# Moving half of an attention product ahead of the output projection, and two ScalarE steps ahead of their neighbours

## The chip, the cores and the metric

The kernel runs on one core of one Trainium2 chip. The metric is the device time of one execution in microseconds (us), and the median of the runs is compared. Profiles come from the hardware profiler and show one execution each. The engines are TensorE (PE; PEld are its weight loads), VectorE (DVE), ScalarE (ACT), GpSimd (POOL) and SyncE (SP).

## What is computed

The input is 16 sequences of 512 tokens with 128 features, in float32. Six blocks follow one another; each works on a layer norm of x. All cases below are per sequence.

```python
x = x + 0.5 * L0_ffn(layernorm(x))        # one 128x128 product and a bias
x = x + L0_attn(layernorm(x))             # retention, 8 heads, group norm, gate
x = x + 0.5 * L0_ffn(layernorm(x))
x = x + 0.5 * L1_ffn(layernorm(x))        # top 256 of 512 tokens through 128-512-128, GELU
x = x + L1_attn(layernorm(x))             # chunked retention, 4 heads
x = x + 0.5 * L1_ffn(layernorm(x))
```

The change is in the part that computes `L1_attn`:

```python
attn = einsum('bhid,bhjd->bhij', qb, kb) * mask
o = einsum('bhij,bhjv->bhiv', attn, vb) + einsum('bhid,bhdv->bhiv', qb * cross_dec, S)
o = o * rsqrt(mean(o * o) + EPS) * gnorm_w
o = (o * silu(g)) @ Wo.T
```

## The kernel before

**Two phases of slots.** `run_slots` (line 57) writes out a software pipeline over the 16 sequences (batches). The first phase (`slot_a`) does the first three blocks and the routed FFN of all batches; one slot, `slot_ab`, joins the phases; the second phase (`slot_b`, g=17 to 31, then `slot_end`) does `L1_attn` and the last routed FFN. Each engine runs its own list of instructions in the order written, and the lists meet in semaphores. Nothing reorders them: the order in each `slot_b` is the schedule.

**A slot of the second phase** handles three batches at once. For the batch *now* it computes scores, the attention product y and the norm of y. For the batch *new* it prepares queries, keys, values and gates (`sl.prepare`). For the batch *old* it does the output projection and the routed FFN (`sl.complete`; slot 17 has no output projection, since no attention of the second phase lies behind it). A sequence is four chunks of 128 tokens.

**PE in a slot** (line 567): the scores of all four chunks and heads (`scores_b`, L287, banks 0 to 3); the transposes of the gated y of *old* (`transpose_gated`, L547, banks X1 and X2); the part of y carried over from the states of earlier chunks (`carry_b`, L334, banks YB and CB); the values' products of chunks 0 and 1 added to it (`attend_b`, L341, which waits for the chunk's masked scores `msk0` to `msk3`); the output projection of *old* (`output_b`, L555, waits for ACT's copy `gt`); in some slots something for the ranking; the transposes of the new x (`ln_ret`, L255, bank 0); chunks 2 and 3 of the values' products; queries and keys (L260, banks 2 and 3), values (L260); the transposes of h, the normalised x2 of *old* (`ln_mod`, L255, bank X1, waits for `ln_mod_xn`); the transposes of y (`transpose_y`, L564, waits for ACT's copy `ycopy`); the gates' product g_mm (L260, banks X1 and X2, so it waits for `ln_mod_xt`, the copy out of X1); the four up-projections of the routed FFN (`routed_up`, L347) around the transposes of queries and keys (L271); the down-projections (`routed_down`, L353 and L356, bank 2); the new states (`states_b`, L303).

A float32 matmul shows as two PE instructions in the profile, so one `attend_b` (four heads) is 8 of them; a transpose shows as one.

**ACT in a slot** (line 818): the copy gt of the gated transposes (L824); the copy of the `ln_ret` transposes to xt_p (L684); the copy of y to qm (L830); `normalise` (L698, h from x2, waits for DVE's nmr); the copy of the `ln_mod` transposes to xt_r (L684); the values (L734); the squares of the transposed y (L838, waits for `ytok`); the gates' tanh (L741); two GELUs (`hidden`, L688); the copy of queries and keys (L747); two GELUs; the copy of the routed FFN's result (L693).

**DVE in a slot** (line 1354): the four masks over the scores (`causal_b`, L1063); in some slots rank work; x2 from the output projection (`scaled_sum`, L1033); its variance (L1006 to L1019); rank work; nmr (L1024, waits for POOL's root L892); the rotation of queries and keys (L1042, L1043, L1049); h added to the base (L1076); rank work in some slots; the head sums over the squares (`head_sums`, L1087, waits for `sq`); the gate (L1351, waits for `tanh`); the router's sum (L1081); the next input and its variance; the norm of y (L1098) and its gating (L1402, signals `gy`, for which the next slot's `transpose_gated` waits); the states' mask (L1069).

**Ranking.** Every eight batches the router's scores are ranked to choose the 256 tokens of each sequence. This is spread over the slots: a HEAD (18, 26), three ROUNDs of two trials each (19 to 21, 27 to 29), a SPLIT (22, 30), and a WEIGH (23, 31). Slots 17, 24 and 25 have none. In a ROUND slot PE adds up a trial (L385) right after `output_b`, and a second one after the keys, for which it waits for DVE.

**`slot_end`** has no *new* batch. It already runs all four `attend_b` in one go before `output_b`. The serial rest of the last ranking and the stores follow it.

Of the kernel before, what the change touches and what calls it, by code (L numbers as in the profile page):

```python
# [8 lines left out]
ACT = mybir.ActivationFunctionType  # L9
# [6 lines left out]
NB, NT = 16, 4  # L16
# [10 lines left out]
BANK = 512  # L27
# [3 lines left out]
YB, CB, X1, X2 = 4, 5, 6, 7  # L31
# [44 lines left out]
def program(nc, x, xt_d, wq0, wk0, wv0, wg0, wo0, gnw, gnb, kern, bias, fa, fb,  # L76
            wq1, wk1, wv1, wg1, wo1, gcol, wr, w1, b1, w2, b2,
            ident_d, cen_d, tri_d, bd0_d, bd1_d, hm_d, rot0_d, rot1_d, blk_d, rs_d, out):
    with ExitStack() as ctx:
        def sb(name, shape, dt=F32):  # L80
            return ctx.enter_context(nc.sbuf_tensor(name, shape, dt))

        def sem(name):
            return ctx.enter_context(nc.semaphore(name))
# [51 lines left out]
        xt = {n: sb(f"xt_{n}", [P, NT, P]) for n in ("p", "c", "r")}  # L136
# [12 lines left out]
        sq = sb("sq", [P, NT * VF])  # L149
# [9 lines left out]
        PS = ctx.enter_context(nc.psum_tensor("ps", [P, 8 * BANK], F32))  # L159
# [23 lines left out]
        s = {n: sem(n) for n in names}  # L183

        def wait(eng, name, count):
            if count > 0:
                eng.wait_ge(s[name], count)
# [64 lines left out]
        def _(pe):  # L252
# [11 lines left out]
            def tiles(k, width=P):  # L264
                return lambda j: bank(k, j * width, width)
# [17 lines left out]
            def scores_b():  # L283
                for c in range(NT):
                    for g in range(G):
                        rows = slice(32 * g, 32 * g + 32)
                        mm = nc.tensor.matmul(bank(g, c * P, P), qkt[rows, 1, c * P:(c + 1) * P],  # L287
                                              qkt[rows, 0, c * P:(c + 1) * P], start=(c == 0), stop=True,
                                              skip_group_check=True)
                mm.then_inc(s["sc01"], 1)  # L290
# [34 lines left out]
            def head(hd, c):  # L325
                at = (YB + hd // 2) * BANK + c * P
                return PS[hd % 2 * V1:(hd % 2 + 1) * V1, at:at + P]
# [10 lines left out]
            def attend_b(c, sl):  # L338
                wait(pe, f"msk{c}", sl.count(0))
                for hd in range(H1):  # L340
                    mm = nc.tensor.matmul(head(hd, c), vv[sl.buf(0)][:, c, hd * V1:(hd + 1) * V1],  # L341
                                          sc[:, c, hd * P:(hd + 1) * P], start=False, stop=True,
                                          skip_group_check=True)
                mm.then_inc(s["y"] if c == NT - 1 else s[f"av{c}"], 1)
# [198 lines left out]
            def transpose_gated(count):  # L543
                wait(pe, "gy", count)
                for k in range(2):
                    for j in range(NT):
                        mm = nc.tensor.transpose(bank(X1 + k, j * P, P),  # L547
                                                 t2[:, j * VF + k * P:j * VF + (k + 1) * P], ident[:])
                mm.then_inc(s["tg"], 1)
# [9 lines left out]
            def transpose_y(count):  # L559
                wait(pe, "ycopy", count)  # L560
                for c in range(NT):
                    for k in range(2):
                        at = YB * BANK + c * VF + k * P
                        mm = nc.tensor.transpose(PS[:, at:at + P], qm[:, k, c * P:(c + 1) * P], ident[:])  # L564
                mm.then_inc(s["ytok"], 1)

            def slot_b(sl):
                now, new, old = sl.count(0), sl.count(1), sl.count(-1)
                g = sl.g
                wait(pe, "ystore", sl.count(-2))  # L570
                if sl.score:
                    wait(pe, "qm", now)
                    scores_b()
                if sl.score:
                    wait(pe, "um", now)
                if sl.complete:
                    transpose_gated(old)
                if sl.score:
                    carry_b(sl)
                    attend_b(0, sl)  # L580
                    attend_b(1, sl)
                if sl.complete:
                    output_b(old)
                if g in HEAD:
                    rank_rows(HEAD[g], X2)
                if g in ROUND:
                    rank_sum(*ROUND[g], X2)
                if g in WEIGH:
                    rank_mask(WEIGH[g], X2)
                if sl.prepare:  # L590
                    if sl.score:
                        wait(pe, "msk3", now)
                    wait(pe, "x1", new)
                    transpose4("ln_ret", x1[sl.buf(1, 4)], 0)
                if sl.score:
                    attend_b(2, sl)
                    attend_b(3, sl)
                if sl.prepare:
                    wait(pe, "ln_ret_xt", new)
                    tilewise(tiles(2), xt["p"], w_qkv1[:, 0:P])  # L600
                    tilewise(tiles(3), xt["p"], w_qkv1[:, P:2 * P], "qk")
                if g in ROUND:
                    rank_sum(ROUND[g][0], ROUND[g][1] + 1, X2)
                if sl.prepare:
                    tilewise(tiles(0, VF), xt["p"], w_qkv1[:, 2 * P:], "v_mm")
                wait(pe, "ln_mod_xn", old)
                transpose4("ln_mod", h, X1)
                if sl.score:
                    transpose_y(now)
                if sl.prepare:  # L610
                    wait(pe, "ln_mod_xt", old)
                    rank_bank(g)
                    tilewise(tiles(X1, VF), xt["p"], w_g1[:], "g_mm")
                    wait(pe, "v", new)
                wait(pe, "ln_mod_xt", old)
                routed_up(0, 1)
                routed_up(1, 0)
                if sl.prepare:
                    transpose_qk(2, new)
                wait(pe, "act0", old)  # L620
                routed_up(2, 1)
                wait(pe, "act1", old)
                routed_up(3, 0)
                if sl.prepare:
                    wait(pe, "qm", new)
                for f in range(NF):
                    routed_down(f, 2, old)
                if sl.prepare:
                    wait(pe, "gate", new)
                    states_b(X1, sl)  # L630
# [50 lines left out]
        def _(act):  # L681
            def copy_xt(st, dst, k, count):
                wait(act, f"{st}_t", count)
                nc.scalar.copy(dst[:].rearrange("p j n -> p (j n)"), bank(k)).then_inc(s[f"{st}_xt"], 1)  # L684
# [10 lines left out]
            def normalise(count):  # L695
                wait(act, "nmr", count)
                for j in range(NT):
                    last = nc.scalar.activation(h[:, j, :], x2[:, j, :], ACT.Identity, bias=nmr[:, j:j + 1],  # L698
                                                scale=rstd["ln_mod"][:, j:j + 1])
                last.then_inc(s["ln_mod_xn"], 1)  # L700
# [117 lines left out]
            def slot_b(sl):  # L818
                now, new, old = sl.count(0), sl.count(1), sl.count(-1)
                if sl.g in HEAD:  # L820
                    route_weight(HEAD[sl.g])
                if sl.complete:
                    wait(act, "tg", old)
                    nc.scalar.copy(gt[:].rearrange("p k n -> p (k n)"), PS[:, X1 * BANK:(X2 + 1) * BANK]) \  # L824
                        .then_inc(s["gt"], 1)
                if sl.prepare:
                    copy_xt("ln_ret", xt["p"], 0, new)
                if sl.score:
                    wait(act, "y", now)
                    nc.scalar.copy(qm[:].rearrange("p k n -> p (k n)"), PS[:, YB * BANK:(YB + 2) * BANK]) \  # L830
                        .then_inc(s["ycopy"], 1)
                normalise(old)
                copy_xt("ln_mod", xt["r"], X1, old)
                if sl.prepare:
                    values_b(sl)
                if sl.score:
                    wait(act, "ytok", now)
                    nc.scalar.activation(sq[:], PS[:, YB * BANK:(YB + 2) * BANK], ACT.Square).then_inc(s["sq"], 1)  # L838
                if sl.prepare:
                    gates_b(sl)  # L840
                hidden(0, 1, old)
                hidden(1, 0, old)
                if sl.prepare:
                    queries_b(sl)
                hidden(2, 1, old)
                hidden(3, 0, old)
                store_y(2, sl.batch(-1), old)
# [694 lines left out]
```

## Time and profile before

| | us |
|---|---|
| median of 3 runs | 887.64 |
| lowest and highest | 887.13, 889.59 |
| the profiled execution's own time | 889.85 |
| its span in the profile | 888.0 |
| PE busy | 781.9 (88%) |
| DVE busy | 738.3 (83%) |
| ACT busy | 408.3 (46%) |
| POOL busy | 429.0 (48%) |

The span is the profiled part of one execution, from its first to its last instruction; 1.85 us of that execution lie outside it. An engine's busy time leaves out its waits. Matmuls overlap, so a group's duration reaches a little into the next group, and the starts are the better marks. The granted clock of PE is 0.967 of full speed on average; DMA carries 20 GB/s.

### The profile page before, as it was taken

The numbers are of one execution on the slowest core, as the hardware profiler recorded it, in microseconds if no ns is written. First come the engines' busy times: TensorE is split into PE (matmuls) and PEld (weight loads), VectorE is DVE, ScalarE is ACT, GpSimd is POOL, SyncE is SP. The second block draws the span as 40 slices with busy tenths as digits, with TensorE's granted clock in tenths as the row PEclk, the third lists the DMA queues.
The fourth block names the chain that finished last, engine by engine and source line by source line (L and its number), as shares of the span: only waits on it lengthen the run. The fifth ranks groups of instructions, "written<-read, shape, count | busy, mean of one in ns | idle before, by whom it ended". The sixth has DMA issues, their size and how long they took to land.

```text
span 888.0 us, 19163 instructions
## 1 busy us (share of the span) xinstructions
PE 781.9 (88%) x7811; PEld 626.8 (71%) x7811; DVE 738.3 (83%) x1915; ACT 408.3 (46%) x803; POOL 429.0 (48%) x300
## 2 busy tenths in 40 slices
PE   2577899999999899998889999999999999999760
PEld 1456688887777677776678777777788778778540
DVE  2668999999999999998777888887778888896667
ACT  0133445455555455444545455555544445555421
POOL 1346777888878676766633333323322323332210
PEclk9798999999999999999999999999999999999885
DMA  7000000000000000000000000000000000000123
GB/s 190 24 25 25 25 25 25 25 26 25 25 24 25 1 25 25 2 25 24 1 1 2 1 1 2 1 1 1 1 2 1 2 1 1 2 1 1 29 67 94
DMA packets 27226, 18.03 MB, mean 20 GB/s; under 512 B 5361, under 2 KB 24706, under 8 KB 26882
## 3 DMA queue, kind: packets, MB, share of 16 engines
q1 hardware_dynamic: 25378, 16.08, 6.1%
q8 instruction: 62, 1.02, 0.5%
q10 hardware_dynamic: 1760, 0.72, 0.4%
q14 instruction: 26, 0.21, 0.1%
HBM read 12.61 MB, written 4.19 MB: 19 GB/s over the span
## 4 chain that ended last, share of the span: by engine, by line
DVE 46%; PE 40%; POOL 6%; issue 3%; ACT 3%; SPq 1%; DMA 0%; DVEq 0%; ACTq 0%; POOLq 0%
PE ps L260 7%; DVE x L1033 6%; PE ps L356 6%; DVE sc L1055 6%; PE ps L347 6%; PE ps L555 4%; DVE st_ln_mod L1006 3%; PE ps L255 2%; DVE st_ln_f L1006 2%; DVE ra L1042 2%; POOL rstd_ln_f L892 2%; PE ps L341 2%; DVE rb L1043 2%; PE ps L547 2%; DVE t L1283 2%
## 5 line engine op out<-in xcount | busy, mean ns | idle before, releaser
L901 POOL TENSOR_TENSOR grstd<-gve,mhalf 128x32 f32<-128x32 f32 (+1 forms) x32 | 133.9, 4184 | 70.4 <-DVE gve L1092 68.7
L347 PE MATMUL ps<-xt_r,w_s 128*128 128x512 f32 x256 | 130.7, 618 | 1.4 <-ACT xt_r L684 1.4
L356 PEld LDWEIGHTS ps<-w_s,hid 128*128 128x128 f32 x1024 | 121.9, 193 | 9.8 <-issue 8.9
L356 PE MATMUL ps<-w_s,hid 128*128 128x128 f32 x1024 | 125.0, 278 | 0.0
L698 ACT ACTIVATE h<-x,nmr,rstd_ln_mod 128x128 f32<-128x128 f32 x128 | 52.7, 482 | 103.1 <-DVE nmr L1024 103.1
L688 ACT ACTIVATE hid<-ps,b_s 128x512 f32<-128x512 f32 x128 | 88.4, 723 | 14.3 <-PE ps L347 14.0
L892 POOL TENSOR_TENSOR rstd_ln_f<-ve_ln_f,mhalf 128x4 f32<-128x4 f32 x32 | 47.9, 1496 | 88.9 <-DVE ve_ln_f L1019 80.4
L1055 DVE TENSOR_TENSOR sc<-ps,tri 128x1024 f32<-128x1024 f32 x64 | 75.3, 1218 | 7.4 <-PE ps L279 6.6
L892 POOL TENSOR_TENSOR rstd_ln_mod<-ve_ln_mod,mhalf 128x4 f32<-128x4 f32 x32 | 32.9, 1027 | 99.7 <-DVE ve_ln_mod L1019 99.7
L260 PE MATMUL ps<-w_qkvg,xt_p 128*128 128x128 f32 x512 | 67.9, 283 | 0.8 <-ACT xt_p L684 0.8
L684 ACT COPY xt_p<-ps 128x512 f32<-128x512 f32 x32 | 18.8, 587 | 104.4 <-PE ps L255 104.4
L260 PEld LDWEIGHTS ps<-w_qkvg,xt_p 128*128 128x128 f32 x512 | 62.2, 196 | 4.5 <-ACT xt_p L684 3.5
L897 POOL TENSOR_TENSOR r_ret<-ve_ret,powers 128x8 f32<-128x8 f32 x32 | 57.6, 1802 | 15.9 <-DVE ve_ret L1019 15.9
L1033 DVE SCALAR_TENSOR_TENSOR x<-ps,r_ret,x 128x128 f32<-128x128 f32 x128 | 36.0, 344 | 34.0 <-PE ps L555 28.2
L260 PE MATMUL ps<-w_qkv,xt_p 128*128 128x128 f32 (+1 forms) x384 | 62.1, 315 | 0.8 <-ACT xt_p L684 0.8
L347 PEld LDWEIGHTS ps<-xt_r,w_s 128*128 128x128 f32 x256 | 44.1, 196 | 24.4 <-issue 14.8
L916 POOL TENSOR_TENSOR rp<-h,wr_b 128x512 f32<-128x512 f32 x32 | 41.5, 1296 | 35.5 <-ACT h L698 35.5
L260 PEld LDWEIGHTS ps<-w_qkv,xt_p 128*128 128x128 f32 x384 | 52.2, 191 | 6.0 <-issue 3.5
L906 POOL TENSOR_TENSOR um<-um 128x128 f32<-128x128 f32 x32 | 14.6, 457 | 76.6 <-DVE um L1069 76.6
L279 PE MATMUL ps<-qm,qkt 32*128 32x256 f32 x512 | 38.0, 411 | 14.7 <-DVE sc L1055 9.4
L1042 DVE TENSOR_TENSOR ra<-ps,rot 128x1024 f32<-128x1024 f32 x32 | 39.0, 1219 | 13.1 <-PE ps L260 13.1
L693 ACT COPY yall<-ps 128x512 f32<-128x512 f32 x32 | 18.8, 587 | 60.8 <-PE ps L356 60.6
(196 smaller groups left out, 1795.6 us busy)
## 6 DMA issues: line engine op xcount, KB each, us to landing
xin<-in_x SPq DMA_DIRECT2D x16, 256.0 KB, 3.0
xtin<-in_xt SPq DMA_DIRECT2D x16, 256.0 KB, 3.4
out_x<-base SPq DMA_DIRECT2D x16, 256.0 KB, 2.4
rot<-in_rot SPq DMA_DIRECT2D x2, 1024.0 KB, 4.8
w_s<-in_w ACTq DMA_DIRECT2D x2, 256.0 KB, 5.9
w_o<-in_wo ACTq DMA_DIRECT2D x1, 128.0 KB
w_qkv<-in_wv SPq DMA_DIRECT2D x1, 128.0 KB
w_g<-in_wg SPq DMA_DIRECT2D x1, 128.0 KB
```

Source lines behind the costliest of these rows:

```text
L260: mm = nc.tensor.matmul(out_at(j), src[:, j, :], w, start=True, stop=True, skip_group_check=True)
L347: nc.tensor.matmul(bank(k), w1_s[:, f, :], xt["r"][:].rearrange("p j n -> p (j n)"), start=True, stop=True).then_inc(s[f"h{f}"], 1)
L356: mm = nc.tensor.matmul(bank(k, j * P, P), hid[:, f, j * P:(j + 1) * P], w2_s[:, f, :], start=False, stop=(f == NF - 1 and j == NT - 1), s ...
L688: nc.scalar.activation(hid[:, f, :], bank(k), ACT.Gelu_apprx_tanh, bias=b1_s[:, f:f + 1]).then_inc(s[f"act{f}"], 1)
L698: last = nc.scalar.activation(h[:, j, :], x2[:, j, :], ACT.Identity, bias=nmr[:, j:j + 1], scale=rstd["ln_mod"][:, j:j + 1])
L892: nc.gpsimd.tensor_tensor(rstd[st][:], ve[st][:], mhalf[:, 0:NT], ALU.pow).then_inc(s[f"{st}_rstd"], 1)
L897: nc.gpsimd.tensor_tensor(r_ret[sl.buf(1, 4)][:], v, powers[:], ALU.pow).then_inc(s["ln_ret_rstd"], 1)
L901: nc.gpsimd.tensor_tensor(grstd[:, 0:n], gve[:, 0:n], mhalf[:, 0:n], ALU.pow) \
L1006: last = nc.vector.bn_stats(st6[st][:, j, :], src[:, j, :])
L1033: last = nc.vector.scalar_tensor_tensor(dst[:, j, :], bank(k, j * P, P), r[:, j:j + 1], src[:, j, :], ALU.mult, ALU.add)
L1042: nc.vector.tensor_tensor(ra[:], qk, rot[:, 0], ALU.mult)
L1055: nc.vector.tensor_tensor(sc[:, c].rearrange("p (b e n) -> p b e n", b=G, e=2), src.rearrange("p b (e n) -> p b e n", e=2), tri[:].rearran ...
```

## The change

In the second phase's `slot_b`, PE makes the values' products of all four chunks in one run, right behind the carried part and ahead of `output_b`; the transposes of y move from behind the `ln_mod` transposes to the place where chunks 2 and 3 were, behind the `ln_ret` transposes. The wait for `msk3` ahead of the `ln_ret` transposes goes, since `attend_b(3)` has waited for it already. ACT copies y ahead of the `ln_ret` copy, and squares the transposed y ahead of `normalise` instead of behind the values. DVE and POOL are untouched, and so are all other slots.

```diff
@@ PE, slot_b
                 if sl.score:
                     carry_b(sl)
-                    attend_b(0, sl)
-                    attend_b(1, sl)
+                    for c in range(NT):
+                        attend_b(c, sl)
                 if sl.complete:
                     output_b(old)
...
                 if sl.prepare:
-                    if sl.score:
-                        wait(pe, "msk3", now)
                     wait(pe, "x1", new)
                     transpose4("ln_ret", x1[sl.buf(1, 4)], 0)
                 if sl.score:
-                    attend_b(2, sl)
-                    attend_b(3, sl)
+                    transpose_y(now)
...
                 wait(pe, "ln_mod_xn", old)
                 transpose4("ln_mod", h, X1)
-                if sl.score:
-                    transpose_y(now)
                 if sl.prepare:
                     wait(pe, "ln_mod_xt", old)
@@ ACT, slot_b
-                if sl.prepare:
-                    copy_xt("ln_ret", xt["p"], 0, new)
                 if sl.score:
                     wait(act, "y", now)
                     nc.scalar.copy(qm[:].rearrange("p k n -> p (k n)"), PS[:, YB * BANK:(YB + 2) * BANK]) \
                         .then_inc(s["ycopy"], 1)
+                if sl.prepare:
+                    copy_xt("ln_ret", xt["p"], 0, new)
+                if sl.score:
+                    wait(act, "ytok", now)
+                    nc.scalar.activation(sq[:], PS[:, YB * BANK:(YB + 2) * BANK], ACT.Square).then_inc(s["sq"], 1)
                 normalise(old)
                 copy_xt("ln_mod", xt["r"], X1, old)
                 if sl.prepare:
                     values_b(sl)
-                if sl.score:
-                    wait(act, "ytok", now)
-                    nc.scalar.activation(sq[:], PS[:, YB * BANK:(YB + 2) * BANK], ACT.Square).then_inc(s["sq"], 1)
```

## Rows read from the trace of the kernel before

**Rows 1.** The page's busy line: us, share of the span, instructions

```profile
PE 781.9 (88%) x7811; PEld 626.8 (71%) x7811; DVE 738.3 (83%) x1915; ACT 408.3 (46%) x803; POOL 429.0 (48%) x300
```

**Rows 2.** Stretches from one `output_b` to the next: us, engines' busy us (instructions), clock, DMA

```profile
578.17:603.42 25.25, 23.57 (x235) 19.19 (x234) 22.16 (x48) 12.61 (x23) 7.71 (x6) 1.00 0.01 2
603.42:627.60 24.18, 23.88 (x239) 19.62 (x238) 18.91 (x43) 12.62 (x23) 7.71 (x6) 1.00 0.00 1
627.60:651.70 24.10, 23.44 (x234) 19.18 (x234) 18.60 (x41) 12.62 (x23) 7.70 (x6) 1.00 0.01 1
799.33:824.40 25.07, 24.76 (x255) 20.51 (x254) 16.50 (x31) 12.62 (x23) 6.09 (x5) 1.00 0.01 2
```

**Rows 3.** Timeline of slot g=24: start, us, engine, line, operation, count, idle before

```profile
629.62 1.13 DVE L1033 SCALAR_TENSOR_TENSOR x<-ps,r_ret,x 128x128 f32<-128x128 f32 x4 [2.33 <-PE ps L555]
...
629.95 1.09 PE L341 MATMUL ps<-sc,va 128*64 128x128 f32 x16
630.05 0.59 ACT L684 COPY xt_p<-ps 128x512 f32<-128x512 f32 x1 [3.24 <-PE ps L255]
...
633.71 1.65 ACT L698 ACTIVATE h<-x,nmr,rstd_ln_mod 128x128 f32<-128x128 f32 x4 [1.61 <-DVE nmr L1024]
...
635.41 0.66 PE L255 MATMUL ps<-ident,h 128*128 128x128 f32 x4 [0.66 <-ACT h L698]
...
635.80 0.91 PEld L564 LDWEIGHTS ps<-ident,qm 128*128 128x128 f32 x8
...
636.10 0.59 ACT L684 COPY xt_r<-ps 128x512 f32<-128x512 f32 x1 [0.75 <-PE ps L255]
...
636.74 1.59 PEld L260 LDWEIGHTS ps<-w_g,xt_p 128*128 128x128 f32 x8
...
638.02 1.05 ACT L838 ACTIVATE sq<-ps 128x1024 f32<-128x1024 f32 x1
...
638.93 1.61 ACT L741 ACTIVATE t<-ps,r_ret 128x256 f32<-128x256 f32 x4
...
646.19 1.23 DVE L1402 TENSOR_TENSOR t<-t,gate 128x1024 f32<-128x1024 f32 x1
...
648.77 1.09 PE L547 MATMUL ps<-ident,t 128*128 128x128 f32 x8
...
649.90 1.01 ACT L824 COPY gt<-ps 128x1024 f32<-128x1024 f32 x1 [2.33 <-PE ps L547]
```

**Rows 4.** Waits from 480 to 800 us: us in total, times, longest

```profile
DVE gve L1087 <- ACT sq L838: 5.6, 9, 0.7
...
PE ps L385 <- DVE rankb L1160: 4.6, 6, 1.1
...
PE ps L255 <- ACT h L698: 3.7, 7, 0.7
```

**Rows 5.** Timeline of the last slot, PE only: the run of all four chunks

```profile
822.43 1.97 PE L341 MATMUL ps<-sc,va 128*64 128x128 f32 x32
```

**Rows 6.** Timeline of slot g=17, which has no `output_b`

```profile
457.77 1.09 PE L341 MATMUL ps<-sc,va 128*64 128x128 f32 x16
...
460.41 3.78 PE L260 MATMUL ps<-w_qkv,xt_p 128*128 128x128 f32 x24
460.52 1.01 ACT L830 COPY qm<-ps 128x1024 f32<-128x1024 f32 x1 [0.45 <-PE ps L341]
```

**Rows 7.** The chain that ended last, in slot g=24: start, us, what

```profile
638.74 1.72 PE ps L347 x4
...
641.33 1.82 PE ps L347 x4
```

**Rows 8.** Timeline of slot g=22, where DVE has rank work

```profile
580.27 1.13 DVE L1033 SCALAR_TENSOR_TENSOR x<-ps,r_ret,x 128x128 f32<-128x128 f32 x4 [0.77 <-PE ps L555]
...
600.44 1.09 PE L547 MATMUL ps<-ident,t 128*128 128x128 f32 x8 [0.94 <-DVE um L1069]
```

**Rows 9.** A stretch of the tail, `routed_up` (L347) alone: PE, PEld busy us, clock, DMA

```profile
852.20:856.10 3.90, 3.78 (x4) 1.17 (x4) 0.51 0.17 50
```

## The prediction, made before the changed kernel was run

> **What bounds the kernel now.** I read the busy line first, then the table of stretches cut at each start of `output_b`, then the timeline of one ordinary slot, then the waits and the chain. TensorE (PE) is busy 88% of the span [rows 1]. The edit touches only the 15 slots of the second phase, g=17 to 31. Cut from one `output_b` to the next they take 24.1 to 25.3 us, with PE busy 23.4 to 24.8 of it and its clock granted in full [rows 2]. So in this phase a microsecond of PE is a microsecond of the kernel, unless PE is waiting there anyway. The places where it waits have to be known exactly.
>
> The slot whose `output_b` starts at 627.60 us (g=24, no rank work) shows them [rows 3]. `output_b` ends about 629.59. From there a chain runs off PE: VectorE (DVE) sums x2 at 629.62, takes its variance, GpSimd (POOL) the root, and ScalarE (ACT) normalises from 633.71 to 635.36. PE has run the `ln_ret` transposes, the products of chunks 2 and 3 (629.95), the queries, keys and values, and still stands idle for 0.66 us before it can transpose h at 635.41. This wait occurs in 7 of the 13 slots of 480 to 800 us; in the six with two rank rounds PE waits instead for DVE's second rank trial, 0.8 us each on average, which also hangs on x2 [rows 4]. Whatever PE does between `output_b` and the transposes of h is therefore not what sets the time: **`output_b` is**. Its end starts the chain, and everything ahead of it in the slot pays in full.
>
> One more place matters. `transpose_y`'s weight loads last from 635.80 to 636.71. ACT's copy of the `ln_mod` transposes out of bank X1 ends at 636.69, and g_mm, which overwrites X1 and waits for that copy, loads its first weights at 636.74 [rows 3]. So today `transpose_y` fills the time of the copy almost to the tenth.
>
> **The change, part by part.**
>
> *Chunks 2 and 3 ahead of `output_b`.* The same 16 PE instructions (two passes for each of eight matmuls) go from behind `output_b` to before it. A run of 16 lasts 1.09 us [rows 3]; one unbroken run of 32, which the last slot already makes, lasts 1.97 [rows 5]. The difference, 0.88, is what lands ahead of `output_b`. The table gives the same in another way: slots 23 and 31 do the same kind of rank work, and what follows 31 has all four chunks ahead of `output_b`. They take 24.18 and 25.07, a difference of 0.89 [rows 2]. I take 0.89. No mask wait is added to it: the two masks of chunks 2 and 3 are ready when PE comes to them, as in the last slot, whose run of 32 shows no idle. ACT's copy gt, for which `output_b` waits, ends at 650.91, 0.79 before `output_b` starts at 651.70, so it does not start to bind [rows 2, 3].
>
> The Trainium skill (TensorE: Matmul & The Clock Gate, Step-by-step: what each phase is for) says that weight loads can be pulled ahead of running matmuls; were every change between kinds of matmul free by that, nothing would be saved by joining two runs, the 16 instructions would cost the full 1.09 wherever they stand, and the sum below would come out at 15.8 instead of 13.0. The trace does not agree: its run of 32 is 0.21 shorter than two runs of 16.
>
> *What this saves behind `output_b`:* nothing. DVE, POOL and ACT need the same time up to h (or up to the rank trial), and PE arrives early today. `transpose_y` takes the place of the products as cover for the `ln_ret` copy: that copy ends 0.69 us after its cover starts (629.95 to 630.64), and `transpose_y` offers 0.94 (635.80 to 636.74) [rows 3]. PE reaches the wait for h about 0.1 sooner and waits 0.1 longer.
>
> *`transpose_y` taken out between the `ln_mod` transposes and g_mm:* also nothing. From 635.41 to 636.74 it is transposes, copy and wake-up, which remain 1.33 us, now with some 0.9 of PE idle. The work has moved to a place that was free, and left a hole where it had been useful.
>
> *y copied first.* In slots 18 to 31 y is complete as `output_b` starts; ACT finished gt before and copies y (1.0 us) while PE spends 2.0 in `output_b`. No wait. What queues behind it on ACT is the `ln_ret` copy, needed only after `output_b`. In slot 17 there is no `output_b`. There PE starts the products at 457.77, so they end 1.97 later, at 459.74, and y's copy runs to about 460.80. `transpose_y`, with 0.95, then holds the queries back from 460.41 to about 461.79: **+1.4** [rows 6]. h isn't late there: squares would end at about 463.0 and the normalising at 464.6, while PE's queries, keys and values, 3.78 us of them, last to 465.6.
>
> *Squares first.* ACT can square about 2.6 us after `output_b` ends and normalises 4.1 after it, so the square of 1.05 fits. It leaves the stretch between values and gates. The gates then wait for g_mm instead, which ends near 638.75 by the pace of its group, against a start at 638.93 now: 0.15 sooner [rows 3]. ACT's first GELUs follow, and the second pair of `routed_up`, which takes 1.82 against 1.72 for the first, should lose that 0.10 of waiting [rows 7]. In the nine slots that are neither paced by DVE nor otherwise late (17, 19, 20, 23 to 25, 27, 28, 31): **-0.9**. DVE starts its head sums up to 0.71 earlier there, but then waits for the gates, so only 0.15 reaches `gy`. `gy` is no limit in an ordinary slot: it ends at 647.42 and PE asks at 648.77 [rows 3].
>
> *The slots where DVE sets the pace* (g=18, 22, 26, 30, those with the longest rank work). In 22 DVE waits 0.77 for `output_b`, then works through to `um`, for which PE idles 0.94 [rows 8]. This chain starts at the end of `output_b`, so the 0.89 counts here as well; the gap before g_mm and the early squares don't.
>
> **Sum.** 14 slots of 0.89 are 12.5; slot 17 adds 1.4; the relief takes 0.9: +13.0. No DMA, POOL or SP instruction is moved. Behind slot 31 comes serial rank work and the stores, which nothing hides, so the sum reaches the end. On the profiled execution (889.85 us outside, span 888.0) this gives 902.9. The median of the three runs is 2.2 below that execution, and I put the forecast on the median: 887.64 + 13.0 = **900.6**.
>
> Bounds: with the moved run at its full 1.09 and no relief it is 14 x 1.09 + 1.4 = 16.7, that is 904.3. If the hole before g_mm turns out 0.1 shorter, as `transpose_y`'s last load may hold g_mm now, 1.5 goes: 899.1.
>
> **Rivals.**
>
> *The DVE-bound slots take the cost in* (897.0). If the four slots with long rank work had slack at `output_b`, 4 x 0.89 = 3.6 would vanish. DVE's 0.77 of idle in front of x2 speaks against it: it waits for PE there, and would wait longer.
>
> *Faster, by the early squares* (about 882). DVE waits 5.6 us for sq in 9 of 13 slots [rows 4]. If head sums, root and `gy` set when the next slot's transposes begin, those 5.6 would come off, and the products moved forward would cost nothing, as PE would be waiting for `gy` anyway. It decides once `gy` comes later than the end of the scores. In ordinary slots it is 1.35 us ahead; where DVE is late, it has no wait for sq to lose.
>
> *The run is hidden anyway* (889.0, no change). Were gt the last thing before `output_b`, 0.79 of each 0.89 would be covered and 0.10 x 14 = 1.4 left. The rows give that 0.79 as slack and not as waiting.
>
> *The clock falls* (927.6). PE gets a hole of 0.9 us in each slot. Four passes of `routed_up`, 1.72 to 1.82 here [rows 7], take 3.78 in the tail where the granted clock is 0.51, that is 1.2 GHz [rows 9]; g_mm at twice its 1.8 in 15 slots would be +27 on top of the 13. But PE had 1.7 us of idle in slot 22's 25.25 and the granted clock stayed 1.00, that is 2.4 GHz [rows 2].
>
> The Trainium skill (TensorE: Matmul & The Clock Gate, What's actually happening) says that the slow clock is the default state and that activity lifts it, so a rule against any order with more idle in it; here the trace shows the idle of slot 22 at full clock.
>
> *Still more is held up* (905 or more): the squares or y's copy hold up `ln_ret`'s copy or h in every slot. The slack of 1.5 us on ACT before h speaks against it.
>
> **How the numbers follow.** The forecast 77%, DVE slots 10%, faster 4%, hidden 3%, clock 3%, more held up 3%. The range takes in the forecast's bounds and the DVE-slot case: 896.5 to 904.3. A change of 0.3%, 2.7 us, is about what a measurement of this kernel can tell from none. Slower by more than that: 77 + 10 + 3 + 3 = 93%; within it 3%; faster 4%.
>
> **What would show it.** In the profile after: one PE run of 32 (L341) of about 1.97 before each `output_b`, a PE idle of 0.8 to 0.9 before g_mm released by ACT's xt_r, the wait for h or for the rank trial a tenth longer, ordinary slots of about 24.9, DVE no longer waiting for sq, the clock still 1.00. The forecast is wrong if h is transposed sooner after `output_b` than 5.8 us, if g_mm starts sooner than 1.3 after these transposes, or if ordinary slots stay at 24.1.

## The result, and the profile after

The changed kernel takes 901.66 us (median of 4 runs, 901.15 to 903.94) against 887.38 beside it: a ratio of 1.0161, 95% interval 1.0137 to 1.0186, or about 14.3 us more. The forecast was 900.6, slower. A second set of runs of both gave 902.49 against 888.03, 1.0156 (1.0132 to 1.0180).

The page of the changed kernel shows nothing of it but the span (the profiled execution took 901.79); the busy line answers to [rows 1]:

```profile
span 900.0 us, 19148 instructions
...
PE 780.8 (87%) x7811; PEld 630.1 (70%) x7811; DVE 736.9 (82%) x1915; ACT 410.8 (46%) x803; POOL 428.4 (48%) x300
```

Every engine does what it did, and 12 us more pass. The stretches from one `output_b` to the next answer to [rows 2] (us, then the busy us of PE, PEld, DVE, ACT and POOL, the granted clock, DMA):

```profile
581.87:607.98 26.11, 23.38 (x235) 19.19 (x234) 21.30 (x46) 12.82 (x23) 7.70 (x6) 1.00 0.01 2
607.98:632.92 24.94, 23.70 (x239) 19.62 (x238) 18.79 (x43) 12.82 (x23) 7.69 (x6) 1.00 0.01 1
632.92:657.79 24.87, 23.26 (x235) 19.18 (x234) 18.50 (x41) 12.83 (x23) 7.69 (x6) 1.00 0.00 1
784.17:810.81 26.64, 24.95 (x234) 20.26 (x234) 21.47 (x46) 12.93 (x23) 7.69 (x6) 0.94 0.01 2
810.81:835.75 24.94, 23.70 (x238) 19.62 (x238) 16.39 (x31) 12.82 (x23) 6.09 (x5) 1.00 0.00 1
```

Slot 24 went from 24.10 to 24.87, slot 23 from 24.18 to 24.94, slot 22 from 25.25 to 26.11. Slot 31, behind which the last slot always had all four chunks ahead of `output_b`, went from 25.07 to 24.94: it alone got shorter. Slot 30 stands out, 26.64 with the clock at 0.94; of that below.

The timeline of slot g=24 (start, duration, engine, line) answers to [rows 3]:

```profile
632.85 2.05 PE L555 MATMUL ps<-w_o,gt 128*128 128x128 f32 x16
632.97 1.01 ACT L823 COPY qm<-ps 128x1024 f32<-128x1024 f32 x1 [1.71 <-PE ps L341]
...
634.94 1.13 DVE L1028 SCALAR_TENSOR_TENSOR x<-ps,r_ret,x 128x128 f32<-128x128 f32 x4 [3.21 <-PE ps L555]
635.07 0.90 PEld L564 LDWEIGHTS ps<-ident,qm 128*128 128x128 f32 x8
...
635.38 0.59 ACT L679 COPY xt_p<-ps 128x512 f32<-128x512 f32 x1 [1.40 <-PE ps L255]
...
636.25 1.02 ACT L829 ACTIVATE sq<-ps 128x1024 f32<-128x1024 f32 x1 [0.29 <-PE ps L564]
...
639.04 1.65 ACT L693 ACTIVATE h<-x,nmr,rstd_ln_mod 128x128 f32<-128x128 f32 x4 [1.76 <-DVE nmr L1019]
...
640.74 0.66 PE L255 MATMUL ps<-ident,h 128*128 128x128 f32 x4 [0.94 <-ACT h L693]
...
641.43 0.58 ACT L679 COPY xt_r<-ps 128x512 f32<-128x512 f32 x1 [0.75 <-PE ps L255]
...
642.07 1.99 PE L260 MATMUL ps<-w_g,xt_p 128*128 128x256 f32 x8 [0.67 <-ACT xt_r L679]
...
644.10 1.57 ACT L736 ACTIVATE t<-ps,r_ret 128x256 f32<-128x256 f32 x4 [0.61 <-PE ps L260]
```

Read it from `output_b`. It starts at 632.92 (the start of its stretch above), and h is transposed at 640.74: 7.82 later. Before, it was 635.41 - 627.60 = 7.81 [rows 2, 3]. (Both marks lie 0.07 behind the first matmul of `output_b`, which starts at 632.85 here and started at 627.53 before.) So nothing that was taken out of this span shortened it; PE's idle ahead of h grew from 0.66 to 0.94. From 640.74 to the first weight load of g_mm, at 642.07 like its first matmul, it is 1.33, as before, now with 0.67 of idle that ACT's xt_r releases. The squares, at 636.25, are long done before normalising. The gates start 3.36 behind the transposes of h, against 3.52 before.

The waits from 480 to 800 us answer to [rows 4] (us in total, times, longest):

```profile
PE ps L260 <- ACT xt_r L679: 7.4, 11, 0.7
...
PE ps L385 <- DVE rankb L1155: 6.3, 6, 1.3
DVE gate L1346 <- ACT t L736: 5.6, 9, 0.7
PE ps L255 <- ACT h L693: 5.6, 7, 1.0
```

DVE's wait for sq is gone, and one for the gates (5.6) has taken its place. PE's waits for the rank trial and for h grew from 4.6 and 3.7 to 6.3 and 5.6, and the hole before g_mm (7.4) is new.

**Where to measure.** The first phase is the same code in all kernels, yet the scores of slot 17 begin anywhere between 451.9 and 456.6 us in the profiled executions. The stretch from the scores of slot 17 to those of the last slot holds exactly what is edited, and repeats better than the whole. The timeline of PE has its two ends, in the kernel before:

```profile
454.73 1.17 PE L287 MATMUL ps<-qkt 32*128 32x128 f32 x32
...
819.49 1.17 PE L287 MATMUL ps<-qkt 32*128 32x128 f32 x32
```

and in the changed kernel:

```profile
453.17 1.17 PE L287 MATMUL ps<-qkt 32*128 32x128 f32 x32
...
830.84 1.17 PE L287 MATMUL ps<-qkt 32*128 32x128 f32 x32
```

So 364.76 became 377.67: **+12.91**. The second profiled execution of the changed kernel gave 377.66. Below, "the stretch" is this span.

### The profile page after: what moved, and what is told of

Its sections match the earlier page's. It is cut to its first block, busy times and chain, and to the rows that moved or that the text cites. A ratio compares the mean times of both kernels' runs of the same rounds, so it can differ in the third digit from the quotient of the medians.

```text
span 900.0 us, 19148 instructions
## 1 busy us (share of the span) xinstructions
PE 780.8 (87%) x7811; PEld 630.1 (70%) x7811; DVE 736.9 (82%) x1915; ACT 410.8 (46%) x803; POOL 428.4 (48%) x300
## 3 DMA queue, kind: packets, MB, share of 16 engines
q8 instruction: 62, 1.02, 0.5%
## 4 chain that ended last, share of the span: by engine, by line
DVE 44%; PE 41%; POOL 6%; ACT 4%; issue 3%; SPq 1%; DMA 0%; DVEq 0%; ACTq 0%; POOLq 0%
PE ps L260 8%; DVE x L1028 6%; PE ps L356 6%; DVE sc L1050 6%; PE ps L347 6%; PE ps L555 4%; PE ps L341 3%; DVE st_ln_mod L1001 3%; POOL rstd_ln_f L887 2%; DVE ra L1037 2%; DVE rb L1038 2%; DVE st_ln_f L1001 2%; PE ps L255 2%; PE ps L547 2%; DVE t L1278 2%
## 5 line engine op out<-in xcount | busy, mean ns | idle before, releaser
L347 PE MATMUL ps<-xt_r,w_s 128*128 128x512 f32 x256 | 129.5, 612 | 1.3 <-ACT xt_r L679 1.3
L683 ACT ACTIVATE hid<-ps,b_s 128x512 f32<-128x512 f32 x128 | 86.5, 702 | 15.7 <-PE ps L347 14.2
L347 PEld LDWEIGHTS ps<-xt_r,w_s 128*128 128x128 f32 x256 | 44.5, 198 | 23.5 <-issue 15.6
L901 POOL TENSOR_TENSOR um<-um 128x128 f32<-128x128 f32 x32 | 14.5, 454 | 85.7 <-DVE um L1064 85.7
```

Of the source, the lines that this page charges most:

```text
L347: nc.tensor.matmul(bank(k), w1_s[:, f, :], xt["r"][:].rearrange("p j n -> p (j n)"), start=True, stop=True).then_inc(s[f"h{f}"], 1)
L683: nc.scalar.activation(hid[:, f, :], bank(k), ACT.Gelu_apprx_tanh, bias=b1_s[:, f:f + 1]).then_inc(s[f"act{f}"], 1)
```

## The experiments

All ran against the kernel before on the same chip. Its median differed a little from set to set: 889.96 beside e1 to e4, 888.03 beside e5 to e8, 889.14 beside e9 to e11. The expectations reckon from about 887.5, so they are best compared with the results by the ratio or by the stretch. The columns are the median, the ratio with its 95% interval, the stretch in the profiled execution and its difference from 364.76.

| run | us | ratio | stretch | difference |
|---|---|---|---|---|
| changed kernel | 901.66 | 1.0161 (1.0137 to 1.0186) | 377.67 | +12.91 |
| e8 changed kernel again | 902.49 | 1.0156 (1.0132 to 1.0180) | 377.66 | +12.90 |
| e1 four ahead, nothing else | 902.64 | 1.0143 (1.0124 to 1.0163) | 377.57 | +12.81 |
| e2 three ahead | 895.09 | 1.0063 (1.0046 to 1.0080) | 371.01 | +6.25 |
| e3 one ahead | 882.94 | 0.9932 (0.9906 to 0.9957) | 358.82 | -5.94 |
| e4 none ahead | 883.67 | 0.9924 (0.9900 to 0.9947) | 356.75 | -8.01 |
| e11 none ahead, again | 882.60 | 0.9930 (0.9911 to 0.9950) | 356.67 | -8.09 |
| e5 transposes and squares early only | 902.53 | 1.0160 (1.0130 to 1.0190) | 378.49 | +13.73 |
| e9 transposes early, squares late | 890.09 | 1.0008 (0.9995 to 1.0021) | 366.21 | +1.45 |
| e6 changed kernel, hole filled | 903.97 | 1.0173 (1.0156 to 1.0190) | 380.25 | +15.49 |
| e7 changed kernel, squares late | 902.38 | 1.0163 (1.0139 to 1.0187) | 378.55 | +13.79 |
| e10 none ahead, gt in halves | 875.80 | 0.9854 (0.9836 to 0.9872) | 352.45 | -12.31 |

Two theories were tested. A, that of the prediction: the end of `output_b` starts the chain that sets the slot, so what stands ahead of it is paid. B: the cost is the hole that `transpose_y` left before g_mm.

**e1, e2, e3, e4: how many chunks stand ahead of `output_b`.** The edit of e1, in PE's `slot_b` alone:

```diff
                     carry_b(sl)
                     attend_b(0, sl)
                     attend_b(1, sl)
+                    attend_b(2, sl)
+                    attend_b(3, sl)
...
                     transpose4("ln_ret", x1[sl.buf(1, 4)], 0)
                 if sl.score:
-                    attend_b(2, sl)
-                    attend_b(3, sl)
+                    pass
```

The wait for `msk3` ahead of the `ln_ret` transposes stays in e1, though the expectation says that it goes; `attend_b(3)` has waited for it already, so it holds nothing up. e2, e3 and e4 keep it too, and put chunks 0 to 2, chunk 0, or none there, and the rest behind the `ln_ret` transposes.

> Only the products of chunks 2 and 3 go ahead of output_b (and the wait for msk3 with them); transposes of y, the y copy and the squares stay where they were before. Theory A (the end of output_b sets the slot; PE idles before h anyway): 14 slots x 0.89 = 12.5, slot 17 +0.5 because the ln_ret copy loses its cover there: 900.4. No idle before g_mm, but the wait for h grows by 0.3 or so. Theory B (the hole before g_mm, left by the transposes of y, is the cost): the transposes of y fill it here, so at most the uncovered ln_ret copy is paid, and the time stays within 887 to 890.

> Chunks 0, 1 and 2 ahead of output_b, chunk 3 behind, everything else as before. Theory A: half of the step, 0.45 in each of 14 slots, 6.2 in all: 893.7. Theory B (hole before g_mm): no hole opens, 887.4.

> The step in the other direction: only chunk 0 ahead of output_b, 1 to 3 behind. Theory A: 0.45 less in each of 14 slots, out of the 0.66 that PE idles before h: 881.2. A rival, that PE's own work bounds the slot and not the chain from output_b: no gain, 887.4.

> All four chunks behind output_b. Theory A: output_b now waits for ACT's copy gt, so it starts 0.67 earlier and not 0.88; in ordinary slots PE reaches h late and only the idle of 0.66 less the new wait of 0.2 is gained, 0.45 a slot; in the four slots paced by DVE 0.67: 10 x 0.45 + 4 x 0.67 = 7.2, 880.2. If the gain went on in a straight line it would be 12.5, 874.9; if PE's work bounds, 887.4 or above.

Measured, by the stretch: +12.81, +6.25, 0 (two ahead, the kernel before), -5.94, -8.01. One chunk is worth 6 us in either direction until none is left. In e3, PE's idle ahead of h in slot 24 has shrunk from 0.66 to 0.22. e1 has no hole before g_mm, and costs the same as the whole change. This settles it against B. The waits of e1 from 480 to 800 us show where the time stands:

```profile
PE ps L260 <- ACT xt_p L685: 8.8, 13, 0.7
PE ps L385 <- DVE rankb L1161: 6.3, 6, 1.3
PE ps L255 <- ACT h L699: 5.7, 7, 1.0
```

PE waits 0.7 in each slot for the `ln_ret` copy, which has lost its cover, and still waits for h and for the rank trial behind that. PE is idle at another place than in the changed kernel, for as long. The new hole is not what e1 pays for: e3 has none, and gains as much for one chunk moved back as one moved forward costs.

e4's last step gives 2.1 instead of 6, as `output_b` now waits for gt. Its timeline:

```profile
624.59 1.01 ACT L824 COPY gt<-ps 128x1024 f32<-128x1024 f32 x1 [2.33 <-PE ps L547]
...
625.66 2.05 PE L555 MATMUL ps<-w_o,gt 128*128 128x128 f32 x16 [0.29 <-ACT gt L824]
...
627.75 1.13 DVE L1033 SCALAR_TENSOR_TENSOR x<-ps,r_ret,x 128x128 f32<-128x128 f32 x4 [1.66 <-PE ps L555]
...
628.08 1.97 PE L341 MATMUL ps<-sc,va 128*64 128x128 f32 x32
```

0.29 us of idle in each slot. I had put this wait at 0.2, and expected -7.2. Slot 24 gains 0.65 (23.45 instead of 24.10 from scores to scores), where I had 0.45: the expectation left out that all four chunks now make one run, which is 0.21 shorter than two. In e4's waits none for h is left, so PE's own work and its wait for gt now bound the ordinary slots.

**e5 and e9: the transposes early.** e5 leaves the products where they were. `transpose_y` goes behind the keys' product (which leaves ACT the time to copy y), and the squares ahead of `normalise`. e9 is the same with the squares back behind the values:

```diff
@@ PE
                     tilewise(tiles(3), xt["p"], w_qkv1[:, P:2 * P], "qk")
+                if sl.score:
+                    transpose_y(now)
...
                 transpose4("ln_mod", h, X1)
-                if sl.score:
-                    transpose_y(now)
@@ ACT, e5 only
+                if sl.score:
+                    wait(act, "ytok", now)
+                    nc.scalar.activation(sq[:], PS[:, YB * BANK:(YB + 2) * BANK], ACT.Square).then_inc(s["sq"], 1)
                 normalise(old)
                 copy_xt("ln_mod", xt["r"], X1, old)
                 if sl.prepare:
                     values_b(sl)
-                if sl.score:
-                    wait(act, "ytok", now)
-                    nc.scalar.activation(sq[:], PS[:, YB * BANK:(YB + 2) * BANK], ACT.Square).then_inc(s["sq"], 1)
```

> The other half of the change alone: chunks 2 and 3 stay behind output_b, the transposes of y move ahead to behind the keys' product, and ACT squares ahead of normalising. Theory A: the transposes take 0.9 out of an idle of 0.66 (before h) or 0.8 (before the second rank trial) and leave a hole before g_mm that the copy needed anyway: about 0.2 in 10 slots, 0.9 in slot 17, less 0.9 of relief by the early squares: 889.4. Theory B (the hole before g_mm is the cost): 15 x 0.9 = 13.5, 901.

That missed by 13 us. Taken alone the number would have spoken for theory B. The chain of slot g=24 in e5 shows what I had overlooked (start, duration, what):

```profile
637.21 0.89 PE ps L564 x8
...
638.12 1.02 ACT sq L834
639.14 1.54 ACT h L698 x4
...
640.73 0.67 PE ps L255 x4
...
641.42 0.59 ACT xt_r L684
```

The squares wait for the transposes, and ACT, which takes its work in order, can't normalise until it has squared. h begins at 639.04 in its timeline, 1.1 later than DVE and POOL allow. Hence e9:

> The run before it (transposes of y and squares early) came out at +14 where 889.4 was expected: in its trace the squares wait for the transposes, which stand behind the keys, and hold normalising up by 1.1 us in a slot. Here the transposes stay early and the squares go back behind the values. If the squares ahead of normalising were the cause, normalising again starts 4.1 after output_b ends, and only the 0.2 in 10 slots and 0.9 in slot 17 remain, with no relief: +3, about 891, and the stretch from the scores of slot 17 to those of the last slot is 368 (before: 364.8; the run before: 378.5). If the hole before g_mm costs its 0.9 after all, it stays at +13, 901.

It came out at +1.45, its ratio no different from 1. Its waits have the hole before g_mm at full size:

```profile
PE ps L260 <- ACT xt_r L684: 7.4, 11, 0.7
...
PE ps L385 <- DVE rankb L1160: 0.2, 1, 0.2
```

7.4 us of idle in 11 slots, the same as in the changed kernel, and it costs almost nothing, because the work that left it filled the idle ahead of h. Of the 1.45, 0.86 is slot 17 (22.35 from scores to scores instead of 21.49), which I had put at 0.9. The ordinary slots 24 and 25 take 24.11 instead of 24.10 and 24.12; the rest is 0.32 to 0.36 more in each of slots 18, 23, 26 and 31, less 0.37 in each of 19 and 27.

**e6: the hole filled.** In the changed kernel, the values of tiles 2 and 3 move behind the transposes of h, where they cover ACT's copy:

```diff
-                    tilewise(tiles(0, VF), xt["p"], w_qkv1[:, 2 * P:], "v_mm")
+                    values_of((0, 1))
                 wait(pe, "ln_mod_xn", old)
                 transpose4("ln_mod", h, X1)
                 if sl.prepare:
+                    values_of((2, 3)).then_inc(s["v_mm"], 1)
                     wait(pe, "ln_mod_xt", old)
```

> The changed kernel, with the second half of the values' product (0.9 us of PE) moved from ahead of the ln_mod transposes to behind them, where it covers ACT's copy. The hole before g_mm closes. Theory A: PE stands idle before h longer instead, by the same amount, and only slot 17 gains: 901.0 (the changed kernel: 901.7). Theory B (the hole is the cost): 14 x 0.8 = 11 less, 890.

No gain, as A has it. The idle moved in front of h (all waits of PE there from 480 to 800 us):

```profile
PE ps L255 <- ACT h L700: 16.0, 13, 1.9
PE ps L385 <- DVE rankb L1162: 6.3, 6, 1.3
```

16.0 us in 13 slots, longest 1.9. Slot 17 gains 0.53 (22.11 against 22.64 in e8), as A has it. But the time is 1.5 higher than that of the changed kernel beside it (e8, below), and the stretch 2.6; slots 28 and 29 are 26.95 and 26.74 from scores to scores, against 25.48 and 25.43 in e8. PE's waits in slot 28, and the stretches of time in which the loss arose, with the granted clock in the third column from the end:

```profile
740.53 0.18 PE L385 MATMUL ps<-rankb,blkb 128*128 128x1 bf16 x1 [1.34 <-DVE rankb L1162]
...
742.41 1.12 PE L255 MATMUL ps<-ident,h 128*128 128x128 f32 x4 [0.73 <-ACT h L700]
```

```profile
741.00:745.00 4.00, 3.27 (x12) 2.51 (x11) 3.96 (x5) 1.94 (x5) 1.27 (x1) 0.65 0.00 0
745.00:750.00 5.00, 5.00 (x22) 3.48 (x21) 2.85 (x5) 4.33 (x11) 2.90 (x1) 0.94 0.01 3
...
770.00:774.00 4.00, 4.00 (x13) 3.21 (x12) 3.61 (x6) 1.92 (x6) 0.51 (x2) 0.64 0.00 0
774.00:777.00 3.00, 3.00 (x14) 1.78 (x13) 1.42 (x2) 3.00 (x7) 2.69 (x1) 1.00 0.00 0
```

The granted clock was 0.65 of full speed over these 4 us, so it stood at 1.2 GHz for part of them and at 2.4 for the rest, and it was back a few us later. It fell behind two waits of PE, for the second rank trial (1.34, in slot 29 0.99) and for h (0.73 in both). It did not fall behind the longest waits: in slot 24 PE waits 1.80 for h in one piece at a clock of 1.00. Slots 28 and 29 together lost 2.8 us. Without that, and without the 0.5 that a fall of the clock cost e8, e6 would be 0.3 above e8: an estimate, and far from the 11 us less that B asks for.

**e7: the squares.** The changed kernel with only the squares put back behind the values.

> The changed kernel with the squares back behind the values. Theory A: the relief of 0.1 in nine slots is lost, 902.6; DVE waits for sq again. A rival, that the early squares bring nothing at all: 901.7. A rival, that they help DVE's chain: above 905.

The median can't tell this apart (902.38 against 902.49 for e8 beside it). The stretch does: 378.55 against 377.66, +0.89. DVE waits for sq again:

```profile
DVE gve L1082 <- ACT sq L833: 5.7, 9, 0.7
```

So the early squares are worth the 0.9 us that the prediction gave them, in one profiled execution of each. Both executions have one fall of the clock, in slot 22, at the same cost (26.64 and 26.63), so it does not enter the difference. The 0.9 lies where the prediction put it: 0.09 to 0.11 in each of slots 17, 19, 20, 23 to 25, 27, 28 and 31, counted from `output_b` to `output_b` (slot 17 from scores to scores), and at most 0.01 elsewhere.

**e8: the changed kernel again.**

> The changed kernel itself, beside the others on the same chip: 901.7, and the interval of slot 30 shows whether its extra 0.5 us and the tail's extra 0.6 us come back: if they do, they belong to the change, if not to the execution.

Slot 30 is ordinary this time: slots 30 and 31 together take 24.94 + 26.10 = 51.04 from scores to scores. But slots 22 and 23 take 26.63 + 24.94 = 51.57, the 0.5 more that slots 30 and 31 had in the first profile. So the extra 0.5 moves from slot to slot and belongs to the execution. Where it sits, the clock had fallen, here as in the first profile. Three stretches of slot 30 there: the one before g_mm, g_mm's and the one behind it:

```profile
790.00:793.30 3.30, 1.70 (x9) 0.99 (x7) 3.10 (x4) 2.19 (x6) 1.35 (x2) 1.00 0.00 0
793.39:796.80 3.41, 3.41 (x9) 2.73 (x10) 3.38 (x4) 1.42 (x4) 0.00 (x0) 0.56 0.00 0
796.80:799.00 2.20, 2.20 (x9) 1.05 (x8) 2.10 (x4) 2.13 (x6) 0.00 (x0) 0.91 0.00 0
```

g_mm takes 3.44 instead of 1.99 there. DVE paces that slot, so all but 0.5 of the loss is hidden: in slot 22 of the same profile PE waits 1.04 for `um` ahead of the transposes of the gated y, in slot 30 not at all. The tail's extra 0.6 came back: behind the scores of the last slot there are 69.2 and 69.1 us in the two executions of the changed kernel, against 68.5 before. But this part, the same code in all kernels, takes anything from 67.7 (e10) to 69.2 (e9, e4) in the profiles, so one or two executions don't show that it belongs to the change.

In steps of 5 us from 460 to 820, the clock stays at 1.00 in the kernel before and in e1, e2, e3, e4, e5, e9 and e11; e10 has one step of 0.95 at its end, in the tail. It falls once in each profile of the changed kernel and in e7, each time behind waits of 1.0 for h and 0.7 for xt_r, and twice in e6, behind the waits shown above. What makes it fall is not shown: slot 22 of the first profile has the same two waits as its slot 30 (1.01 and 0.67) at 1.00, slots 19 to 21 and 27 of e6 have the same 0.99 and 0.73 as its slot 29 at 1.00, and e5 waits for h and then for xt_r in every slot from 18 on (0.4 to 0.9, then 0.7) without a fall.

**e10: better than both.** e4 leaves one wait, for gt. ACT now copies bank X1 and bank X2 one after the other, and `output_b` takes the first half of each token's features for all four tiles, then the second. The start flag stands on the first matmul into the bank alone, instead of once for each tile. All four chunks stand behind `output_b`, as in e4. The edit against e4:

```diff
@@ ACT
-                    nc.scalar.copy(gt[:].rearrange("p k n -> p (k n)"), PS[:, X1 * BANK:(X2 + 1) * BANK]) \
-                        .then_inc(s["gt"], 1)
+                    for k, name in ((0, "gt_half"), (1, "gt")):
+                        nc.scalar.copy(gt[:, k, :], bank(X1 + k)).then_inc(s[name], 1)
@@ PE, in place of output_b
+                wait(pe, "gt_half", sl.k)
+                for k in range(2):
+                    if k == 1:
+                        wait(pe, "gt", sl.count(-1))
+                    for j in range(NT):
+                        mm = nc.tensor.matmul(bank(X1, j * P, P), gt[:, k, j * P:(j + 1) * P], w_o1[:, k, :],
+                                              start=(k == 0 and j == 0), stop=(k == 1), skip_group_check=True)
+                mm.then_inc(s["wo"], 1)
```

> All four chunks behind output_b, where PE waits 0.27 for gt in each slot. ACT copies gt in two halves (bank X1, then X2), and output_b takes all four tiles' first halves, then the second ones, so it can start when the first copy is done. Theory A: the wait goes, 0.27 in 14 slots, 3.8 less than with one copy: the stretch from the scores of slot 17 to those of the last slot 353 instead of 356.8, the time near 879. If ACT's second copy comes late or PE is bound elsewhere: no gain.

> All four chunks behind output_b, once more beside the version with two copies: stretch 356.8 as before, ratio to the kernel before 0.991 to 0.993.

The stretch is 352.45, 4.2 less than e11's 356.67, and the time 875.8: 13 us below the kernel before beside it, whose median was 889.14; by the ratios it is 3% below the changed one. Its timeline in slot 24:

```profile
621.84 0.89 PE L334 MATMUL ps<-qkt,um 64*64 64x128 f32 x24
621.95 1.07 ACT L835 COPY gt<-ps 128x512 f32<-128x512 f32 x2 [2.33 <-PE ps L547]
...
622.66 2.05 PE L565 MATMUL ps<-w_o,gt 128*128 128x128 f32 x16
...
624.75 1.12 DVE L1043 SCALAR_TENSOR_TENSOR x<-ps,r_ret,x 128x128 f32<-128x128 f32 x4 [1.31 <-PE ps L565]
...
625.07 1.97 PE L341 MATMUL ps<-sc,va 128*64 128x128 f32 x32
```

`output_b` starts 0.82 behind the carried part, with no idle of PE. Two copies of 512 columns take 1.07 together, against 1.01 for one of 1024. The median dropped by more (6.8 against e11) than the stretch. The two profiled executions differ by 4.3, like the stretch; the other 2.5 are not explained.

## Why the prediction was right

- **The sum.** It was worked out for the part from slot 17 on as +13.0; the stretch gave +12.91 and +12.90. That the two are so near is in part luck. Both profiles contain about 0.5 us of a fall of the clock, which the sum had put at nothing. Without it 12.4 are left, 0.6 less than the sum: its largest term, 14 slots of 0.89, measured 0.86 each, 12.0 instead of 12.5, and slot 17 a little less than 1.4. The medians moved by 14.3, in an interval of 12.2 to 16.5, which holds both the 13.0 and the 12.9; what they moved beyond the stretch is not explained. The two profiled executions differ by only 11.9, since the first phase was 1.6 us longer in the one before (454.73 against 453.17), though its code is the same.
- **0.89 ahead of `output_b`.** Confirmed in place, and nearly in size: +0.85 to +0.86 from `output_b` to `output_b` in slots 18, 21, 22, 26 and 29, and 0.76 to 0.77 in 19, 20, 23 to 25, 27 and 28, where the relief comes off. That a run of 32 is 0.21 shorter than two of 16 decided between 13.0 and 15.8. The Trainium skill (TensorE: Matmul & The Clock Gate, Step-by-step: what each phase is for) says that weight loads are pulled ahead of running matmuls. That every change between kinds of matmul is free by this was my own extension of it, and the 0.21 speaks against it here.
- **Nothing saved behind `output_b`.** From the start of `output_b` to the transposes of h it is 7.82 against 7.81. This was the step on which the sign depended, and e1 to e4 confirm it by moving the run and nothing else. PE's extra wait for h was mis-sized, 0.28 (0.94 less 0.66) where the prediction has 0.1, but as idle it costs nothing.
- **The hole before g_mm is free.** 1.33 before and after; e9 and e6 show it from both sides.
- **Slot 17.** 22.64 from scores to scores against 21.49: +1.15, where the working gives 1.4 less 0.1.
- **The squares.** e7 against e8 gives 0.10 a slot in the nine slots named, and 0.89 in all for the predicted 0.9. DVE's gain was taken up by a wait for the gates, as predicted.
- **The DVE-paced slots** pay in full: +0.86 in slot 22. That rival falls.
- **The clock.** The rival had 3% and a price of 27 us for a fall in each slot, and the forecast expected a clock of 1.00 throughout. That is wrong in a detail: the clock does fall, but once in 15 slots, at a cost of 0.5 us in a slot that DVE paces (in e6 1.5 and 1.3 in slots 28 and 29). I had taken slot 22's idle at full clock as reason enough. The Trainium skill (TensorE: Matmul & The Clock Gate, What's actually happening) says that activity lifts the slow clock. The direction agrees: each fall in these profiles came behind waits of PE, and the clock rose again with PE busy. Why one slot in 15 falls and the others, with the same waits, do not stays open.

What I got wrong lies behind the prediction: in e5 I moved ACT's squares without asking what they wait for and who is queued behind them. Without e9, e5's number would have spoken for theory B by accident.

## What to carry to other kernels

Find where the chain that sets the period leaves the busiest engine, here at the end of `output_b`, and look at both sides of it. Work ahead of that point costs its full length and work behind it is free until the chain's answer is waited for, however full the engine looks in total; so the same products that cost 12.8 us when moved forward brought 8.0 when moved back, and 12.3 once the next wait, for gt, was gone too. An engine that takes its work in order must not be given an early step whose input comes late, as e5's squares did.

## What the runs showed that I had not expected

- The granted clock fell in the middle of a phase in which PE was 93% busy: 0.56 over 3.4 us in slot 30 of the changed kernel, right after PE had waited 1.02 for h and 0.68 for xt_r (g_mm 3.44 instead of 1.99). It came back within the slot. In e1 PE idles as much, at other places, and in e5 at the same places, and the clock stays at 1.00.
- One unbroken run of 32 small matmuls takes 1.97, against 1.09 for each of two runs of 16 (the weight loads stand idle 0.17 before each of these runs and behind it). Four chunks in one run take 1.97 wherever they stand: ahead of `output_b` in the changed kernel, behind it in e4.
- DVE and POOL can hold each other up, and in these cases the instruction that starts later gets longer. In the kernel before, DVE's L1049 starts 0.54 behind POOL's product (L916) in slot 24 and takes 1.82, against 1.22 in slots 17 and 21, where POOL does nothing beside it; POOL's product keeps its 1.28. It is not so with every pair: in the last slot of the kernel before, adding h to the base (L1076) runs beside POOL's L901 and takes 0.69, and it takes 0.68 in the ordinary slots. In slot 24 of e5 L1049 comes first and keeps 1.22, POOL's product starts beside it and takes 1.76, and L1076, which starts beside that, takes 1.76:

```profile
640.75 1.76 POOL L916 TENSOR_TENSOR rp<-h,wr_b 128x512 f32<-128x512 f32 x1 [3.08 <-ACT h L698]
641.31 1.76 DVE L1076 SCALAR_TENSOR_TENSOR base<-h,x 128x512 f32<-128x512 f32 x1
```
